# Blank rows for the whole area of the experts' rows, written during attention; reciprocals one reduce later

## The chip, the cores and the metric

The kernel runs on one core of a Trainium2 chip. The metric is the device time of one execution in microseconds (us); less is better. The times before come from three timed runs, the profile from one more execution that was recorded.

## What is computed

The reference is a gated cross-attention followed by a gated mixture of experts, in float32, over 16 slices of 128 rows with 512 columns:

```python
x = x + jnp.tanh(g_xattn[0]) * _L0_xattn_ref(_layernorm(x), ctx, ctx, gamma)
x = x + jnp.tanh(g_ffn[0])   * _L0_ffn_ref(_layernorm(x), ...)

# attention: B=16, 8 heads of 16 rows, 512 queries and 512 keys each
sm = softmax(einsum('bhdq,bhdl->bhql', qh, kh) / sqrt(16)); ret = einsum('bhql,bhdl->bhdq', sm, vh)

# experts: 2048 tokens, 8 experts of hidden size 256..1024, the best 2 of each token
h = x @ down_w + down_b
logits = x @ router_w + router_b - COST_LAMBDA * cost
topv, topi = top_k(softmax(logits), 2); gate = softmax(topv)
out = sum over the two of gate * (gelu(gelu(h * mask) @ w1 + b1) @ w2 + b2)      # every expert's constant term counts
out = (out + 0.1 * shared(h)) @ up_w + up_b + (gelu(x) @ core_w + core_b)
```

## The kernel before

**Attention.** It runs in windows `w`, one for each of the 16 slices, and three more at the ends, here numbered by `w`. In a window TensorE makes 16 score blocks `nat` (L536), the k-th of 0 to 15; VectorE takes the maximum of each (`tensor_reduce`, L707) and, between two of those, does the small jobs of the table `PLACED` (L663): the normalization's statistics of the next slice, the reciprocals `rc` of the softmax sums of two slices ago (L696, behind k = 5), and the statistics of x1. ScalarE takes the exponentials (L632), GpSimd all the slice-wide arithmetic. Windows 4 to 13 are a hardware loop whose body holds two windows.

SyncE issues nearly every transfer of attention, in the order of `sync.body`, from one hardware queue: a transfer waits in program order behind all that stands before it. A window's order is: X (L408), the softmax sums to DRAM (L440), a piece of the weights of 800 KB (L420), the sums back as `dc` (L446), xr, ctx (L416), the k rows to scratch (L467, L468), the k stack of head group 0 from scratch (L396), the reciprocals to scratch (L466), the q rows to scratch, the reciprocals spread (L477), the q stack of group 0 (L396), u and x1 rows out, both stacks of group 1, a block of zeros for the experts' sums (L1177). Each read from scratch waits for the landing of what was written to scratch. The stacks of group 0 have to be in place before the next window's first `nat`.

**Feed-forward.** Four rounds r = 0 to 3 of four slices each: TensorE transposes, multiplies by `down_w`, the router, the shared expert and the core; VectorE selects the two experts of each token and ranks it, and GpSimd scatters each token's row of 1088 bytes to its place in `g_rows` with indirect DMAs (L2042, eight in a round). `g_rows` has for each of the 8 experts a region of 2304 rows, and behind them the unused block of 256 rows. The order on each engine is the hand-written list in `seq`. In the last round the totals of the experts come out of a small matmul (`tot`, L1388) as `nz` (L1571), from which VectorE works out tables of 42 blocks (L1786 to L1878): which rows (`ro`), which weights (`wo`), which biases (`bo`).

An expert's last block of 256 rows reaches past its tokens. So that these rows are harmless (zeros, with an index that adds to rows nobody reads), SyncE writes 256 blank rows behind each expert's count: `fillers` (L1199), eight times a register load of the count `nz` and a DMA of 272 KB, and once for the unused block (L1214). The blank rows stand in `u`, which VectorE clears at the start of the last round (L1976, L1978).

**Expert blocks.** For each of 42 blocks SyncE loads 256 rows transposed (L1240) and their meta columns (L1244); first it waits for `ro`, then in `all_rows_out` for every scatter and blank write. TensorE makes two layers of matmuls (L1295), ScalarE GELU (L1641), VectorE the low parts and the gates, GpSimd adds the rows to `y_sums`. ScalarE's first step there waits for all stores of xb (`t_xs`, L1630). At the end the sums are read back, multiplied by `up_w` and stored.

## Time and profile before

| | |
|---|---|
| timed runs | 732.62, 732.62, 734.15 us; median 732.62 us |
| profiled execution, device time | 740.14 us |
| its span, first to last instruction | 738.0 us |
| busy share: TensorE, VectorE, ScalarE, GpSimd | 93%, 71%, 73%, 65% |
| granted TensorE clock, mean | 0.995 of full speed |
| moved by DMA | 123.98 MB, 168 GB/s |

Stages on the span's clock: lead-in to about 15 us, attention to about 370 us, the four rounds to about 475 us, expert blocks to about 700 us, the end to 738 us. The profiled execution is 7.5 us longer than the median of the timed ones; 2.1 us of it lie around the span, which each execution has some of.

### The profile page before, as it was taken

What the parts mean: (1) busy time and instruction counts of PE and PEld (TensorE: products, weight loads), DVE (VectorE), ACT (ScalarE), POOL (GpSimd) and SP (SyncE); (2) the same over time, 40 slices, a digit from 0 to 9 for tenths busy, and PEclk for the clock granted to TensorE, in tenths of its full rate; (3) what the DMA queues carried; (4) which work ended last, traced back from release to release, by engine and by line L of the source; (5) the groups of instructions that cost most, each with busy time, mean ns of one, the idle gap of its engine ahead of it and who ended that gap; (6) DMA issues with size and microseconds to landing.
All of it is one profiled execution on the core that took longest, in us unless ns stands there. A gap on an engine that the chain in (4) does not pass through costs nothing.

```text
span 738.0 us, 20869 instructions
## 1 busy us (share of the span) xinstructions
PE 687.9 (93%) x6101; PEld 373.1 (51%) x6101; DVE 525.0 (71%) x853; ACT 541.0 (73%) x1129; POOL 480.7 (65%) x474
## 2 busy tenths in 40 slices
PE   1799998999999999999989999799999999999988
PEld 0122222232333333322355544588888888888744
DVE  3989998899999999998877756544444444444456
ACT  2399999899999999999885665487676666767411
POOL 3558788888888898985477244046666666656623
PEclk9999999999999999999999999999999999999999
DMA  6656666656655666545255635599988888887487
GB/s 201 199 151 196 199 207 217 197 175 208 209 192 186 208 207 220 177 139 182 93 166 182 210 118 175 147 172 174 126 119 121 118 135 106 108 102 94 56 250 277
DMA packets 136865, 123.98 MB, mean 168 GB/s; under 512 B 70612, under 2 KB 106196, under 8 KB 136792
## 3 DMA queue, kind: packets, MB, share of 16 engines
q1 hardware_dynamic: 121928, 106.58, 50.4%
q0 software_dynamic: 13632, 15.47, 14.7%
q10 hardware_dynamic: 1232, 0.98, 0.5%
q8 instruction: 41, 0.67, 0.4%
q14 instruction: 32, 0.26, 0.1%
HBM read 60.33 MB, written 51.53 MB: 152 GB/s over the span
## 4 chain that ended last, share of the span: by engine, by line
PE 71%; DVE 10%; DMA 7%; issue 5%; ACT 3%; SPq 3%; POOL 1%; ACTq 0%; DVEq 0%; POOLq 0%
PE EH L1295 25%; PE Y L1295 16%; PE pv L561 12%; PE ring L548 8%; DVE mx L707 6%; PE nat L536 5%; ACT P L632 2%; DMA k_scratch<-khl 1%; DMA QS<-mrow 1%; DVE statx L688 1%; PE ring L580 1%; DMA q_scratch<-qhl 1%; SPq L396 1%; PE ring L571 1%; DMA y_sums<-ysb,to 1%
## 5 line engine op out<-in xcount | busy, mean ns | idle before, releaser
L707 DVE TENSOR_REDUCE mx<-nat 128x2 f32<-128x1024 f32 x256 | 296.8, 1213 | 23.2 <-PE nat L536 22.3
L632 ACT ACTIVATE P<-ring 128x512 f32<-128x512 f32 x512 | 279.4, 603 | 19.8 <-PE ring L548 9.8
L2091 POOL DMA_INDIRECT y_sums<-ysb,to x84 | 138.4, 1647 | 101.6 <-DVE ysb L2028 88.5
L561 PE MATMUL pv<-P,VT 128*32 128x256 f32 x2048 | 158.7, 394 | 0.4
L536 PE MATMUL nat<-KS,QS 48*128 48x512 f16 x512 | 111.8, 397 | 24.4 <-DMA QS<-q_scratch 15.1
L548 PE MATMUL ring<-QS,KS 49*128 49x512 f16 x512 | 123.5, 392 | 9.1 <-ACT P L632 8.5
L1641 ACT ACTIVATE X<-EH,bcur 128x256 f32<-128x256 f32 x168 | 85.6, 559 | 50.9 <-DVE u L1992 27.0
L1295 PE MATMUL Y<-whi,u 128*128 x672 | 117.1, 273 | 0.5 <-DVE u L1992 0.5
L1295 PE MATMUL EH<-XA,whi 128*128 128x256 f16 x672 | 116.9, 273 | 0.3 <-DMA XA<-g_rows 0.3
L1992 DVE TENSOR_TENSOR u<-X,u 128x512 f16<-128x512 f32 x84 | 57.7, 687 | 78.3 <-ACT u L1647 76.5
L1295 PE MATMUL Y<-wlo,u 128*128 x336 | 91.6, 273 | 0.0
L1295 PE MATMUL EH<-XA,wlo 128*128 128x256 f16 x336 | 91.6, 273 | 0.0
L561 PEld LDWEIGHTS pv<-P,VT 128*32 128x32 f32 x2048 | 44.2, 109 | 91.7 <-issue 45.4
L548 PEld LDWEIGHTS ring<-QS,KS 49*128 49x128 f16 x512 | 32.4, 93 | 112.3 <-ACT P L632 95.6
L1295 PEld LDWEIGHTS Y<-whi,u 128*128 128x128 f16 x672 | 65.7, 98 | 8.8 <-issue 1.3
L1295 PEld LDWEIGHTS EH<-XA,whi 128*128 x672 | 65.7, 98 | 8.5 <-issue 1.0
L2028 DVE TENSOR_TENSOR ysb<-Y,gcur 128x512 f32<-128x512 f32 x42 | 29.0, 691 | 46.6 <-PE Y L1295 46.6
L1647 ACT CAST u<-X 128x512 f16<-128x512 f32 x84 | 51.9, 618 | 7.3 <-ACT X L1641 0.4
L536 PEld LDWEIGHTS nat<-KS,QS 48*128 48x128 f16 x512 | 26.0, 94 | 37.7 <-DVE mx L707 21.5
L1295 PEld LDWEIGHTS Y<-wlo,u 128*128 128x128 f16 x336 | 32.9, 98 | 3.8
L1295 PEld LDWEIGHTS EH<-XA,wlo 128*128 x336 | 32.9, 98 | 3.8
L1655 ACT CAST uh<-Y 128x256 f16<-128x256 f32 x16 | 6.0, 372 | 32.3 <-PE Y L1508 32.3
(266 smaller groups left out, 995.4 us busy)
## 6 DMA issues: line engine op xcount, KB each, us to landing
XA<-in_wall SPq DMA_DIRECT2D x8, 800.0 KB, 4.4
u<-in_wall SPq DMA_DIRECT2D x8, 800.0 KB, 4.4
QS<-q_scratch SPq DMA_DIRECT2D x64, 96.0 KB, 2.5
KS<-k_scratch SPq DMA_DIRECT2D x62, 96.0 KB, 2.2
X<-in_x SPq DMA_DIRECT2D x16, 256.0 KB, 2.8
q_scratch<-qhl SPq DMA_DIRECT2D x16, 256.0 KB, 2.1
xr<-in_x SPq DMA_DIRECT2D x16, 256.0 KB, 3.7
rd<-den_scratch SPq DMA_DIRECT2D x16, 256.0 KB
```

The costliest lines, as they stand in the source:

```text
L396: sp.dma_start(dst[HALF * a:HALF * a + K_QK, g, :, :], src).then_inc(t_stk[g][b % 2].sem, 16)
L536: m = pe.matmul(nat[k % 2][:, a, :], QS[i][r, g, n, q0:q0 + P], KS[i][r, g, n, :], start=True, stop=True)
L548: pe.matmul(ring[place[key] % 3][:, :], KS[i][r, g, n, lb * P:lb * P + P], QS[i][r, g, n, :], start=True, stop=True).then_inc(t_ring.sem, 1)
L561: m = pe.matmul(pv[32 * j:32 * j + 32, q], VT[i][:, lb, g, j, :], Pb[4 * (s % 2) + j][:, q], start=(lb == 0 and half == 0), stop=(lb == 3) ...
L632: act.activation(Pb[4 * (s % 2) + j][:, :], bank[:, :], ACT.Exp).then_inc(t_use.sem, 1)
L707: dve.tensor_reduce(mx[:, k // 8, :, k % 8], nat[k % 2][:, :, :], AX.X, ALU.max).then_inc(t_max.sem, 1)
L1295: m = pe.matmul(dst, l, r, start=first and n == 0, stop=last and n == 2, skip_group_check=skip)
L1641: m = act.activation(af[j % 2][:, tile, :], EH[j % 2][:, n, s * BLK:(s + 1) * BLK], ACT.Gelu, bias=bcur[:, j % 2, tile:tile + 1], scale=bc ...
L1647: act.copy(ah[j % 2][:, 2 * n:2 * n + 2, :], af[j % 2][:, 2 * n:2 * n + 2, :]).then_inc(t_ah.sem, 1)
L1992: dve.tensor_tensor(al[j % 2][:, 2 * n:2 * n + 2, :], af[j % 2][:, 2 * n:2 * n + 2, :], ah[j % 2][:, 2 * n:2 * n + 2, :], ALU.subtract).th ...
L2028: dve.tensor_tensor(ysb[j % 2][:, :, :], EY[j % 2], gcur[:, j % 4, :].unsqueeze(2).broadcast_to([P, 2, LAT]), ALU.mult).then_inc(t_dve.sem, 1)
L2091: pool.indirect_dma_start(out=ysum[:, :], out_offset=bass.IndirectOffsetOnAxis(ap=to[:, j % 2, a:a + 1], axis=0), in_=ysb[j % 2][:, a, :], ...
```

## The change

The blank rows move from `u` into a tile of their own, `blank` (two rows of 1088 bytes in each partition, 2176 bytes), of which `zs` and `Z` become parts. GpSimd clears it at the very start in place of `zs`; in window 2 a small DMA writes the two index columns, which now come from the constants. In each of the windows 3 to 14 SyncE writes 1536 rows of `g_rows` in two halves of 128 x 3 x 2176 bytes (816 KB each): half 0 between the k rows' stores and the k stack of group 0, half 1 at the window's end. After 12 windows all 18432 rows of the eight regions are blank; window 15 writes the unused block (272 KB). `fillers`, the block write of L1214 and VectorE's clearing in the last round are gone; the scatters of round 0 wait for all blank writes (`t_zr`), and so does the first later use of `zs` as something else. The reciprocals go from behind k = 5 to behind k = 6, ahead of x1's statistics, both behind the same reduce.

```diff
-            "gb": sb("gb", [P, NT]), "zs": sb("zs", [P, LAT]), "Z": sb("Z", [P, LAT]),
+            "gb": sb("gb", [P, NT]), "blank": sb("blank", [P, ROW]),
         }
+        keep["zs"], keep["Z"] = (keep["blank"][:, k * ROW // 2:k * ROW // 2 + LAT] for k in range(2))
...
                     sp.dma_start(scr[ck.index(b), :, 2], hl[b % 2][:, high, :]).then_inc(t_.sem, 16)
+                    if side == 1 and 3 <= w < B - 1:
+                        tail["blank rows"](ck, w, 0)
                     if side == 1:
                         stack(ck, b, 0, 1)
...
             if 3 <= w < B:
                 tail["zeros"](ck, w)
+            if 3 <= w < B - 1:
+                tail["blank rows"](ck, w, 1)
+            if w == B - 1:
+                tail["unused block"]()
...
-        PLACED = {1: ("stats",), 2: ("aggr",), 5: ("recip",), 6: ("xstats",), 7: ("xaggr",)}
+        PLACED = {1: ("stats",), 2: ("aggr",), 6: ("recip", "xstats"), 7: ("xaggr",)}
...
-                    if todo and (todo[0][1] in PLACED.get(k, ())):
+                    while todo and todo[0][1] in PLACED.get(k, ()):
...
-                pool.memset(keep["zs"][:, :], 0.0).then_inc(t_vt.sem, 1)
+                pool.memset(keep["blank"][:, :], 0.0).then_inc(t_vt.sem, 1)
...
-    blank = flat(u)[:, 0:ROW].rearrange("p (a c) -> p a c", a=2)
+    blank = keep["blank"][:, :].rearrange("p (a c) -> p a c", a=2)
+    by_window = gsc[0:DUMP, :].rearrange("(w h j p a) c -> w h p j (a c)", h=2, j=3, p=P, a=2)
...
+        def blank_in():
+            sp.dma_start(blank[:, :, LAT:LAT + META],
+                         const[:, NCONST + K2_BLANK:NCONST + K2_BLANK + 2 * META].rearrange("p (a c) -> p a c", a=2)).then_inc(t_bl.sem, 16)
+
+        def blank_rows(ck, w, half):
+            if w == 3:
+                sp.wait_ge(t_bl.sem, 16)
+            sp.dma_start(by_window[ck.index(w - 3), half],
+                         blank[:, :, :].rearrange("p a c -> p (a c)").unsqueeze(1).broadcast_to([P, 3, ROW])).then_inc(t_zr.sem, 16)
+
+        def unused_block():
+            sp.dma_start(gsc[DUMP:DUMP + BLK, :].rearrange("(p a) c -> p (a c)", a=2),
+                         blank[:, :, :].rearrange("p a c -> p (a c)")).then_inc(t_zr.sem, 16)
...
-            def fillers():
-                wait(sp, t_act, NG - 1, "nz", 0)
-                for e in range(E):
-                    v = sp.value_load(nz[0:1, e:e + 1], min_val=0, max_val=ROWS)
-                    region = gsc[e * REGION:(e + 1) * REGION, :]
-                    sp.dma_start(blocks(region[bass.ds(v, BLK), :]), blank).then_inc(t_zr.sem, 16)
...
-                if r == NG - 2:
-                    sp.wait_ge(t_zd.sem, 10)
-                    sp.dma_start(blocks(gsc[DUMP:DUMP + BLK, :]), blank).then_inc(t_zr.sem, 16)
...
-                    if r == NG - 2 and t == 0:
-                        fillers()
...
-                sp.wait_ge(t_zr.sem, 16 * (E + 1))
+                sp.wait_ge(t_zr.sem, t_zr.value)
...
                         act.wait_ge(t_dz.sem, t_dz.value)
+                        act.wait_ge(t_zr.sem, t_zr.value)
...
-                if r == NG - 1:
-                    wait(dve, t_pe, 2, "uT", LB - 1)
-                    dve.memset(blank, 0.0).then_inc(t_zd.sem, 1)
-                    dve.wait_ge(t_zd.sem, 9)
-                    dve.tensor_copy(blank[:, :, LAT + META - 1], cs2[:, K2_DUMP:K2_DUMP + 2]).then_inc(t_zd.sem, 1)
...
+                if (r, i) == (0, 0):
+                    pool.wait_ge(t_zr.sem, t_zr.value)
```

On SyncE's queue, window 3 from its ctx load to the loop's start. Before:

```order
L416 DMA X<-in_ctx_kv 128x512
L467 DMA k_scratch<-khl 128x1024
L468 DMA k_scratch<-khl 128x512
L396 DMA KS<-k_scratch 48x2x512 x2
L466 DMA den_scratch<-rc 128x32
...
L396 DMA QS<-q_scratch 48x2x512 x2
L1174 DMA y_sums<-zs 128x2x256 x2
L1177 DMA y_sums<-zs 128x256 x4
L377 UNCONDITIONAL_BRANCH
```

After (`y_sums<-blank` is the same write of zeros, out of the new tile):

```order
L417 DMA X<-in_ctx_kv 128x512
L468 DMA k_scratch<-khl 128x1024
L469 DMA k_scratch<-khl 128x512
L1198 DMA g_rows<-blank 128x3x544
L397 DMA KS<-k_scratch 48x2x512 x2
L467 DMA den_scratch<-rc 128x32
...
L397 DMA QS<-q_scratch 48x2x512 x2
L1186 DMA y_sums<-blank 128x2x256 x2
L1189 DMA y_sums<-blank 128x256 x4
L1198 DMA g_rows<-blank 128x3x544
L378 UNCONDITIONAL_BRANCH
```

Two transfers of 816 KB have come in, one behind the k rows' stores and one behind the zeros; nothing else has changed places.

On VectorE, window 3 from the next slice's statistics on. Before:

```order
L682 BN_STATS stats<-X 128x6
L707 TENSOR_REDUCE mx<-nat 128x2
L685 BN_AGGR mv<-stats 128x2
L707 TENSOR_REDUCE mx<-nat 128x2 x3
L696 RECIPROCAL rc<-dc 128x32
L707 TENSOR_REDUCE mx<-nat 128x2
L688 BN_STATS statx<-ao 128x6
L707 TENSOR_REDUCE mx<-nat 128x2
L692 BN_AGGR mvx<-statx 128x2
```

After:

```order
L691 BN_STATS stats<-X 128x6
L716 TENSOR_REDUCE mx<-nat 128x2
L694 BN_AGGR mv<-stats 128x2
L716 TENSOR_REDUCE mx<-nat 128x2 x4
L705 RECIPROCAL rc<-dc 128x32
L697 BN_STATS statx<-ao 128x6
L716 TENSOR_REDUCE mx<-nat 128x2
L701 BN_AGGR mvx<-statx 128x2
```

The reciprocal has moved behind one more reduce and stands directly ahead of x1's statistics.

## Rows read from the trace of the kernel before

**Rows 1.** Two stretches: length, engines' busy us, granted clock, DMA share, GB/s

```profile
40.00:345.00 305.00, 292.16 (x2896) 90.03 (x2893) 288.06 (x300) 282.35 (x584) 253.51 (x285) 0.99 0.61 194
500.00:600.00 100.00, 100.00 (x918) 89.63 (x917) 43.11 (x76) 69.63 (x154) 63.10 (x39) 1.00 0.88 131
```

**Rows 2.** A group of DMA issues: count, KB each, us to landing, the page

```profile
XA<-in_wall SPq DMA_DIRECT2D x8, 800.0 KB, 4.4
```

**Rows 3.** VectorE in one window of the loop: start, us, line, what

```profile
252.78 0.34 DVE L696 RECIPROCAL rc<-dc 128x32 f32<-128x32 f32 x1
...
255.93 11.41 DVE L707 TENSOR_REDUCE mx<-nat 128x2 f32<-128x1024 f32 x10
267.25 0.69 DVE L682 BATCH_NORM_STATS2 stats<-X 128x6 f32<-128x512 f32 x1
```

**Rows 4.** SyncE's queue in the same window: start, us of issue, line, transfer

```profile
247.05 0.34 SPq L420 DMA_DIRECT2D XA<-in_wall  x1
248.01 0.34 SPq L446 DMA_DIRECT2D dc<-den_scratch  x1
...
259.39 0.84 SPq L396 DMA_DIRECT2D QS<-q_scratch  x2
```

**Rows 5.** Stretches of the same window, columns as in rows 1

```profile
246.00:248.00 2.00, 2.00 (x23) 0.63 (x17) 1.89 (x3) 1.81 (x5) 1.90 (x3) 1.00 0.16 60
248.00:254.00 6.00, 6.00 (x60) 1.98 (x60) 5.25 (x7) 5.57 (x14) 5.08 (x9) 1.00 0.87 293
254.00:255.00 1.00, 1.00 (x13) 0.21 (x5) 1.00 (x3) 0.86 (x3) 0.76 (x2) 1.00 0.00 0
```

**Rows 6.** SyncE's queue in window 4, the loop's first

```profile
100.95 0.34 SPq L446 DMA_DIRECT2D dc<-den_scratch  x1
...
113.16 1.14 SPq L396 DMA_DIRECT2D QS<-q_scratch  x2
```

**Rows 7.** VectorE in window 4; in brackets its idle us and what ended it

```profile
104.35 0.35 DVE L696 RECIPROCAL rc<-dc 128x32 f32<-128x32 f32 x1 [0.25 <-DMA dc<-den_scratch]
...
117.63 2.36 DVE L707 TENSOR_REDUCE mx<-nat 128x2 f32<-128x1024 f32 x2 [0.98 <-PE nat L536]
```

**Rows 8.** Stretches of window 4, columns as in rows 1

```profile
98.00:101.00 3.00, 3.00 (x29) 1.04 (x28) 2.97 (x4) 2.82 (x8) 2.85 (x4) 1.00 0.45 121
101.00:106.00 5.00, 5.00 (x52) 1.51 (x52) 4.01 (x5) 4.58 (x11) 3.99 (x9) 1.00 0.92 324
```

**Rows 9.** The last round, SyncE: blank writes (all eight, and one alone), first load

```profile
451.32 13.76 SPq L1203 DMA_DIRECT2D g_rows<-u  x8
...
460.31 0.00 SPq L1203 DMA_DIRECT2D g_rows<-u  x1
...
472.39 1.37 SPq L1240 DMA_TRANSPOSE XA<-g_rows  x1
```

**Rows 10.** The last round, VectorE

```profile
458.34 0.57 DVE L1800 TENSOR_TENSOR hc<-hc 128x8 f32<-128x8 f32 x3
464.75 0.75 DVE L1920 SCALAR_TENSOR_TENSOR X<-EH,gate,X 128x512 f32<-128x512 f32 x1 [5.84 <-PE Y L1409]
```

**Rows 11.** The chain that ended last, in order of time: start, us, what

```profile
456.27 5.18 PE EH L1295 x24
...
463.60 1.09 issue
464.69 5.36 PE EH L1295 x24
...
471.84 1.28 DVE sal L1902 x2
...
474.94 2.83 DMA xb_rows<-X
...
479.03 1.03 ACT X L1641 x2
```

**Rows 12.** A stretch of the last round, columns as in rows 1

```profile
458.00:465.00 7.00, 5.68 (x34) 3.14 (x33) 1.02 (x6) 0.97 (x2) 3.84 (x4) 1.00 0.59 199
```

## What the change should do, and why

> **What bounds the kernel now.** I read the stretches first [rows 1]. In attention TensorE, VectorE and ScalarE are all busy for 93 to 96% of 305 us, and the DMA engines for 0.61: what is added to an engine there costs at once, while transfers have room, as long as nobody waits for one that stands behind them. In the expert blocks TensorE alone is full (100.00 of 100.00 us). So the 9 small writes that go were never part of a full engine's work, and the question is where a transfer's end releases someone: in attention the order of SyncE's queue [rows 4, 6], in the last round the path from the counts to the first expert block [rows 9 to 11].
>
> **The size of what comes.** A half is 128 x 3 x 2176 bytes = 816 KB, as much as a piece of the weights (800 KB), which takes 4.4 us from issue to landing [rows 2]. Over 5 us in which the queue is never empty the core moves 324 GB/s at a share of 0.92 [rows 8], so 0.836 MB take 0.836 / 324 x 1000 = 2.6 us at that pace, and 2.4 us at a full share. Two halves in 12 windows are 20.1 MB against 2.5 MB that go. In a window of 20.7 us this is 4.8 us more, 0.23 of share: 0.61 becomes 0.84. They fit on average.
>
> **Half 1 in a window of the loop.** It stands ahead of the sums' store, whose landing SyncE awaits before it reads dc. The DMA engines are nearly idle from 246 to 248 (share 0.16), 1.7 us, just where half 1 would run [rows 5]. Of 2.4 us some 0.7 are left over, plus about 0.5 us for one more issue (an issue takes 0.34 to 0.45 us here [rows 4]) and 0.5 for X and the sums that move behind it: dc is issued some 1.7 us later than 248.01 and lands that much later at the most. The reciprocal at 252.78 did not wait; behind k = 6 it stands one reduce later, and a reduce takes 1.14 us here (11.41 / 10), so at about 254.2 with the gaps [rows 3], 1.4 us later. Since the dc packets stood behind 800 KB of weights anyway, the delay is less than the issue's. I take no wait; the bounds are 0 and 0.5 us a window.
>
> **Half 0 in a window of the loop.** It stands behind the k rows' stores and ahead of the k stack. The DMA engines are idle from 254 to 255 (share 0.00) while the k rows' landing is awaited [rows 5]: 1 us of 2.4 is free, about 1.4 us pass to the k stack and the q rows, less what their own waits give back. The q stack is issued at 259.39 + 0.84 [rows 4]. It is needed at the next window's k = 0: ten reduces from 255.93 to 267.25 at 1.14 each, of which the last two are the next window's, so at 265.0 [rows 3]. Even with the 4.4 us of the 800 KB piece it lands at 264.6; small reads take less. 1.4 us fit. Cost 0, with the same bound of 0.5 us a window.
>
> **Window 4 is different.** There the q stack is late already: VectorE waits 0.98 us for the first `nat` and starts at 117.63, and the reciprocal waits 0.25 us for dc [rows 7]. The reason is window 3, which writes six blocks of zeros at once: SyncE issues dc at 100.95, sits on the landings of what stands behind it, and issues the q stack only at 113.16 [rows 6]. Half 1 of window 3 stands behind those zeros. From 98 to 101 the share is 0.45 [rows 8], so 1.65 us are free, of which I count 1.2 (the rest comes after dc's turn); 1.2 us stay, and 0.5 of issue. Half 0 of window 4 runs while the k rows' landing is awaited, at no cost but an issue. So the q stack is 1.0 to 1.7 us later and nothing hides it, since it is the last to arrive: **+1.3 us, once**. The reciprocal there would stall some 0.5 us; it lies ahead of the same wait and is not added. Bounds: 0 (if the stores come through sooner) and +2.6 (a full half).
>
> **The reciprocals.** Moved, not added: 0.34 us stay 0.34 us. In windows 15 and later its store to scratch stands behind it on SyncE, but also behind 2 MB of loads; nothing.
>
> **The waits that come.** ScalarE before `zs` is overwritten and GpSimd before the first scatter wait for writes issued 25 us earlier: 0. GpSimd's first clearing grows from 256 to 544 columns, a few tenths in the lead-in beside VectorE's chain: 0 to +0.3, I take 0.1.
>
> **The last round.** VectorE's clearing (some 0.6 us) at its start is beside TensorE's matmuls: 0. SyncE's part is more: eight reads of the counts with a write each from 451.32 for 13.76 us [rows 9]. Their end is not awaited by the load at 472.39, which comes 2 us behind `ro`. But during them something odd stands in the trace. VectorE is done with `hc` at 458.91 and should go on with the core's sum of the second slice, whose 12 matmuls are the first half of the 24 from 456.27 and end at 458.9 [rows 10, 11]; it starts at 464.75, after 5.84 us [rows 10], put down to a matmul that is not its own. ScalarE and SyncE too go on only then, and TensorE has 1.09 us of idle with no releaser up to 464.69 [rows 11]. The DMA engines are at 0.59 meanwhile [rows 12]: it is no lack of bandwidth. If it goes with the fillers, then: TensorE starts its 24 matmuls at 463.60 in place of 464.69 and ends them at 469.0; `sal`, which stands 7.1 us behind 464.75 in VectorE's own order (471.84), would stand at 466.1 by that, or at 467 where ScalarE decides, so before 469.0; the last two steps of the shared expert follow without their wait from 470.05 to the end of the first `sal` at 472.5, so 1.1 + 2.4 = 3.5 us are won on TensorE [rows 11]. ScalarE's wait for the last xb store (474.94 + 2.83) moves with TensorE and VectorE by 4 to 4.5 us, and so does its first GELU at 479.03. The first output matmuls stand behind both and come some 3.8 us earlier, and from there TensorE is full: **-3.8 us**, bounds -3.5 and -4.5. If it does not go, or stands only in the recorded execution: 0.
>
> Whether the timed runs have this halt the profile can't say. The profiled execution is 7.5 us longer than their median, and a halt with all its effects is 4 to 6 us of just this sort. Within it SyncE's write at 460.31 stands with 0.00 us, where an issue takes 0.34 us and more [rows 4, 9]: that looks like records held up, not like work. So I take it as part of the recording. The Trainium skill bears on it from both sides. "NOTIFIC — the notification-queue block", section 7.1, says that the block that writes a profile's records holds engines up rather than lose a record inside it; by that the halt is the recorder's, no row here shows the block itself, and the timed gain is nothing. "Runtime: NRT & Kernel Launch", section on the preamble and postamble, gives a gap of about 6.2 us between a profile's total and the execution time for any kernel; an estimate by that page leaves 1.3 us of the 7.5 for the halt, which would then be real and the gain nearly whole. The two disagree, and no run here decides.
>
> **The sum.** Window 4 +1.3, lead-in +0.1, last round -0.2 (SyncE and the DMA engines less loaded, no row that a full engine waits on): +1.2 us. The median 732.6 becomes **733.8 us**. In the recording the halt should go as well: 740.1 + 1.2 - 3.8 = 737.5.
>
> **The rivals.**
> - The halt is real and the fillers make it. Then 732.6 + 1.3 + 0.1 - 3.8 = 730.2; with both bounds 728.2 to 731.7. For it: three engines stand still at once in the span in which SyncE does the count reads. Against it: a shorter one stands in the round before, without fillers, and the above.
> - The other side: the halves also cost in each window of the loop, through dc or the q stack. It decides from the point at which a landing comes later by more than the 1.4 us that the reciprocal gained, or the q stack by more than the 2 us and more up to 265.0. VectorE then stands in 10 to 11 windows for 0.3 to 1 us: +3 to +10, with window 4 about 739 us. For it: a mean share of 0.84 lengthens every landing. Against it: the gaps above.
> - The change does nothing measurable: window 4's wait is absorbed by later idle time of others, or the blank halves run where nobody waits: 732.5.
>
> **Chances.** Forecast (733.0 to 735.3) 0.50: about two thirds of it within 0.2%, which is 1.5 us and about what a measurement of this kernel can tell from no change, the rest above. Halt real and gone 0.28, of which 0.24 is faster by over 0.2%. Cost in each window 0.14, all slower. Nothing 0.08. So faster 0.24, within 0.2% 0.43 (0.32 of the forecast, 0.04 of the halt, 0.07 of nothing), slower 0.33. The range that holds 8 in 10 goes from 729.4 to 737.5: it takes in nearly all of the real halt and the lighter end of the cost in each window. The likeliest case has 733.0 to 735.3 of its own.
>
> **What would show it.** After, VectorE's idle time before the first reduce of window 5 should be 2 to 3 us, and once; elsewhere the reciprocal should have no DMA as its releaser. The DMA share of attention should be 0.80 to 0.86. The core's sum on VectorE behind `hc` should come within 0.3 us. If it does and the timed runs are about 4 us faster, the halt was real and my step on the recording is wrong. If attention's stretch grows by more than 3 us, the gaps were misread.

## The result and the profile after

The changed kernel takes **739.78 us** in the median of four runs (738.32 to 740.94), the kernel before 733.38 us beside it: ratio 1.0092, interval 1.0076 to 1.0108. It is 6.4 us slower. I had forecast 733.8 us with 737.5 as the upper end, so the time lies outside the range, on the side of the rival that costs in attention. The recorded execution has a device time of 738.32 us and a span of 736.1 us. That is shorter than the 740.14 us recorded for the kernel before, and both signs are explained below.

The columns of the stretches are those of [rows 1]. The first line is attention, the second the expert blocks:

```profile
40.00:345.00 305.00, 288.58 (x2836) 87.99 (x2832) 282.94 (x296) 276.89 (x572) 248.45 (x281) 0.98 0.79 258
...
500.00:600.00 100.00, 100.00 (x918) 89.63 (x917) 43.21 (x77) 69.05 (x152) 63.32 (x39) 1.00 0.91 131
```

In the same 305 us TensorE is busy 3.6 us less than in [rows 1], VectorE 5.1 us less, ScalarE 5.5 us less, and the DMA share is 0.79 where it was 0.61. The expert blocks are as before. So attention lost time. Its end can be read from one row of each kernel, all 256 reduces of VectorE (shortest/median/longest in ns, first and last start in us); before stands first, then after:

```profile
L707 DVE TENSOR_REDUCE mx<-nat x256: 1162/1217/1228, 14.4 to 346.4; 128x2 f32<-128x1024 f32 x128
```

```profile
L716 DVE TENSOR_REDUCE mx<-nat x256: 1160/1215/1229, 14.2 to 351.6; 128x2 f32<-128x1024 f32 x128
```

The last start is 5.2 us later. The statistics of the next slice stand in each window behind k = 1 and serve as a clock. VectorE before, windows 4 to 8:

```profile
97.86 0.68 DVE L682 BATCH_NORM_STATS2 stats<-X 128x6 f32<-128x512 f32 x1
119.91 0.68 DVE L682 BATCH_NORM_STATS2 stats<-X 128x6 f32<-128x512 f32 x1
142.17 0.68 DVE L682 BATCH_NORM_STATS2 stats<-X 128x6 f32<-128x512 f32 x1
163.23 0.68 DVE L682 BATCH_NORM_STATS2 stats<-X 128x6 f32<-128x512 f32 x1
184.38 0.68 DVE L682 BATCH_NORM_STATS2 stats<-X 128x6 f32<-128x512 f32 x1
```

VectorE after, the same with the reciprocals, in brackets the idle time and what ended it:

```profile
97.82 0.68 DVE L691 BATCH_NORM_STATS2 stats<-X 128x6 f32<-128x512 f32 x1
107.98 0.35 DVE L705 RECIPROCAL rc<-dc 128x32 f32<-128x32 f32 x1 [2.79 <-DMA dc<-den_scratch]
122.76 0.68 DVE L691 BATCH_NORM_STATS2 stats<-X 128x6 f32<-128x512 f32 x1
144.39 0.68 DVE L691 BATCH_NORM_STATS2 stats<-X 128x6 f32<-128x512 f32 x1
151.93 0.35 DVE L705 RECIPROCAL rc<-dc 128x32 f32<-128x32 f32 x1 [0.89 <-DMA dc<-den_scratch]
168.15 0.68 DVE L691 BATCH_NORM_STATS2 stats<-X 128x6 f32<-128x512 f32 x1
188.87 0.68 DVE L691 BATCH_NORM_STATS2 stats<-X 128x6 f32<-128x512 f32 x1
```

Window 4 takes 24.94 us in place of 22.05, window 6 takes 23.76 in place of 21.06; windows 5 and 7 are 0.63 and 0.43 us shorter than before. That makes 4.5 us at window 8, and 0.7 us come later. In this record the loss is not spread over the loop: it sits in two windows, and in both VectorE stands at the reciprocal for `dc`, which is late. The kernel before is not the whole measure, though. With the reciprocals alone moved (`recip_only` below) window 4 takes 23.49 us and window 6 takes 20.71, and attention ends at 345.9. Beside that kernel the blank rows cost 5.7 us of attention, 1.45 of them in window 4 and 3.05 in window 6.

**How `dc` becomes late.** SyncE in window 4, start and us of issue:

```profile
97.47 0.46 SPq L1198 DMA_DIRECT2D g_rows<-blank  x1
...
99.09 1.89 SPq L441 DMA_DIRECT2D den_scratch<-U  x2
101.35 0.35 SPq L421 DMA_DIRECT2D u<-in_wall  x1
103.45 0.33 SPq L447 DMA_DIRECT2D dc<-den_scratch  x1
```

Half 1 of window 3 is the first line. `dc` is issued at 103.45 where [rows 6] has 100.95: 2.5 us later, about the whole transfer of a half. The chain that ended last goes through just this:

```profile
100.43 2.75 DMA den_scratch<-U
103.45 4.42 DMA dc<-den_scratch
108.89 1.13 DVE mx L716
110.45 1.39 PE pv L570 x16
```

**What the wait sets off.** TensorE, with its idle time in brackets, and two stretches:

```profile
110.06 0.39 PE L545 MATMUL nat<-KS,QS 48*128 48x512 f16 x2 [2.99 <-DVE mx L716]
...
113.05 1.08 PE L570 MATMUL pv<-P,VT 128*32 128x256 f32 x8
...
114.72 0.64 PE L570 MATMUL pv<-P,VT 128*32 128x256 f32 x8
```

```profile
111.00:115.00 4.00, 4.00 (x37) 0.71 (x25) 2.72 (x4) 1.85 (x4) 3.67 (x4) 0.58 0.49 160
152.00:156.00 4.00, 2.59 (x23) 0.83 (x24) 4.00 (x6) 2.62 (x6) 2.72 (x6) 0.91 1.00 349
156.00:160.00 4.00, 4.00 (x26) 0.67 (x24) 2.73 (x3) 2.38 (x5) 3.62 (x4) 0.50 0.51 163
```

The reduces stand behind the reciprocal in VectorE's order and the next `nat` behind the reduces, so TensorE stands for 2.99 us. Then its granted clock falls: eight `pv` matmuls take 1.08 us in place of 0.64, and the mean over 111 to 115 us is 0.58. In window 6 the wait is only 0.89 us, but TensorE was busy for 2.59 of 4 us and from 156 to 160 it runs at 0.50, the lower level of 1.2 GHz. Window 6 is 2.7 us longer than before, three times the wait. What the clock alone costs can be read from two of the kernels below, `both` and `half1_only`, of which each waits once for `dc` in its window 12, 1.89 and 1.79 us. The stretch behind the wait, `both` first:

```profile
284.00:288.00 4.00, 4.00 (x49) 1.25 (x41) 4.00 (x5) 2.91 (x6) 3.58 (x4) 1.00 0.49 158
```

```profile
284.00:288.00 4.00, 4.00 (x25) 0.67 (x24) 2.85 (x3) 2.55 (x5) 3.52 (x4) 0.50 0.51 161
```

With the clock at 1.00 the window takes 22.96 us, with the fall to 0.50 it takes 25.09, 2.1 us more for a wait that is no longer. So a wait of a given length has no one price: whether the clock falls behind it decides, and these records do not show what decides that.

**The last round.** The core's sum behind `hc` on VectorE, as in [rows 10]:

```profile
461.91 0.57 DVE L1815 TENSOR_TENSOR hc<-hc 128x8 f32<-128x8 f32 x3
462.51 0.75 DVE L1935 SCALAR_TENSOR_TENSOR X<-EH,gate,X 128x512 f32<-128x512 f32 x1
```

The halt of 5.84 us is gone. The span is 1.9 us shorter although attention ends 5.2 us later, so 7.1 us are won behind attention. They go with the halt and not with the fillers as such: `recip_only`, which has all the fillers and in its record no halt, takes 384.6 us from the last reduce's start to the end of its span, the changed kernel 384.5, the kernel before 391.6. The recorded executions differ by +5.2 and -7.1 us, the timed ones by +6.4.

### The profile page after: what moved, and what is told of

Same layout as the page of the kernel before. It is cut to its first block, busy times and chain, and to the rows that moved or that the text cites. A ratio compares the mean times of both kernels' runs of the same rounds, so it can differ in the third digit from the quotient of the medians.

```text
span 736.1 us, 20885 instructions
## 1 busy us (share of the span) xinstructions
PE 688.5 (94%) x6101; PEld 372.8 (51%) x6101; DVE 524.8 (71%) x851; ACT 541.1 (74%) x1129; POOL 481.1 (65%) x474
## 4 chain that ended last, share of the span: by engine, by line
PE 76%; DVE 9%; DMA 5%; issue 4%; SPq 3%; ACT 2%; POOL 0%; DVEq 0%; ACTq 0%; POOLq 0%
PE EH L1309 27%; PE Y L1309 17%; PE pv L570 13%; PE ring L557 9%; DVE mx L716 6%; PE nat L545 5%; ACT P L641 2%; DMA k_scratch<-khl 1%; DMA dc<-den_scratch 1%; PE ring L589 1%; DVE statx L697 1%; SPq L397 1%; DMA q_scratch<-qhl 1%; PE ring L580 1%; DMA QS<-q_scratch 1%
## 5 line engine op out<-in xcount | busy, mean ns | idle before, releaser
L749 POOL TENSOR_TENSOR ao<-tn,rd 128x512 f32<-128x512 f32 x16 | 20.3, 1269 | 14.8 <-DMA rd<-den_scratch 14.7
```

Source lines behind the costliest of these rows:

```text
L749: done(pool.tensor_tensor(ao[i][:, :], tn[:, :], rd[:, :], ALU.mult))
```

## The experiments

Each session timed its kernels beside the kernel before. Medians differ between sessions (before: 733.5, 732.9, 738.8, 738.1 and 733.6 us), so ratios are read within one. "Last reduce" is the last start of the row quoted twice above, from the recorded execution, which for each kernel of this table is one of its timed runs.

| kernel | last reduce, us | median, us | ratio to before | interval | before |
|---|---|---|---|---|---|
| recip_only | 345.9 | 732.75 | 0.9990 | 0.9972 to 1.0008 | 733.53 |
| both | 352.9 | 739.47 | 1.0082 | 1.0055 to 1.0110 | 733.53 |
| half0_only | 346.7 | 732.66 | 0.9985 | 0.9966 to 1.0004 | 733.53 |
| half1_only | 355.1 | 737.55 | 1.0061 | 1.0038 to 1.0083 | 733.53 |
| half1_moved | 358.6 | 743.79 | 1.0152 | 1.0121 to 1.0184 | 732.87 |
| recip_at_8 | 348.9 | 738.35 | 1.0079 | 1.0056 to 1.0102 | 732.87 |
| dc_first | 358.2 | 745.28 | 1.0155 | 1.0119 to 1.0192 | 732.87 |
| moved_dc_first | 378.9 | 765.08 | 1.0436 | 1.0405 to 1.0467 | 732.87 |
| late_zeros | 342.9 | 734.97 | 0.9942 | 0.9914 to 0.9969 | 738.75 |
| after_late_zeros | 349.1 | 739.59 | 0.9998 | 0.9965 to 1.0031 | 738.75 |
| on_scalar_queue | 382.2 | 768.87 | 1.0381 | 1.0329 to 1.0433 | 738.75 |
| tiny_halves | 346.0 | 737.89 | 1.0001 | 0.9972 to 1.0029 | 738.75 |
| window3_spared | 349.2 | 738.97 | 1.0013 | 0.9988 to 1.0037 | 738.08 |
| recip_at_5 | 354.6 | 743.28 | 1.0077 | 1.0044 to 1.0110 | 738.08 |
| zeros_only | 345.8 | 734.24 | 0.9948 | 0.9923 to 0.9973 | 738.08 |
| after_again | 350.4 | 739.58 | 1.0030 | 1.0004 to 1.0056 | 738.08 |
| reads_kept | 354.5 | 738.50 | 1.0073 | 1.0047 to 1.0098 | 733.57 |
| writes_kept | 353.6 | 740.09 | 1.0082 | 1.0055 to 1.0108 | 733.57 |

### One part at a time

The reciprocals alone, on the kernel before:

```diff
-        PLACED = {1: ("stats",), 2: ("aggr",), 5: ("recip",), 6: ("xstats",), 7: ("xaggr",)}
+        PLACED = {1: ("stats",), 2: ("aggr",), 6: ("recip", "xstats"), 7: ("xaggr",)}
```

> The kernel before, with the reciprocals behind k = 6 as in the changed kernel and nothing else changed. Theory (a wait of VectorE for the softmax sums `dc` is what costs in attention, through TensorE behind it and its clock): the two waits of the reciprocal in windows 4 and 5 (0.25 and 0.78 us in the trace of before) go, and with them the dip of the granted clock at 128 to 136 us; TensorE's 1.37 us of lag at 133 us is won, so 0.7 to 1.5 us faster than before, and attention in the record 0.7 to 1.5 us shorter. Rival (the move of the reciprocals is itself what lengthens attention, by holding GpSimd's normalization back): slower than before by 1 to 5 us.

The other three are the changed kernel with the fillers put back beside the blank rows of attention (`both`), and of that only half 0 or only half 1 in each window:

```diff
 # both; half0_only also leaves out the second call, half1_only the first
+            def fillers():
+                wait(sp, t_act, NG - 1, "nz", 0)
+                for e in range(E):
+                    v = sp.value_load(nz[0:1, e:e + 1], min_val=0, max_val=ROWS)
...
+                    sp.dma_start(blocks(region[bass.ds(v, BLK), :]), late_blank).then_inc(t_zf.sem, 16)
-                        tail["blank rows"](ck, w, 0)
-                tail["blank rows"](ck, w, 1)
```

> The changed kernel with the fillers of the kernel before put back as well (eight reads of the counts with a write of 272 KB each, the unused block, VectorE's clearing of `u`), beside the blank rows of attention. Theory (the halt of 5.84 us belongs to that one recorded execution and the fillers cost nothing where nothing is recorded): as the changed kernel, 739.8 us, within 1 us. Rival (the halt is real, and its removal paid back a part of what attention costs): 3.8 to 6.8 us slower than the changed kernel, 743.5 to 746.5 us. For both attention in the record is about 5 us longer than before.

> As the kernel before this one in the list (fillers kept), but without half 1 in each window, so half of the area gets blank rows only from the fillers, as in the kernel before. Theory (half 1 ahead of the sums' stores makes `dc` late): `dc` is issued as early as before, the reciprocals do not wait, attention is within 1 us of the one with the reciprocals alone moved, and the time 732 to 734.5 us. Rival (it is the load on the DMA engines, whatever the place): half of the loss, about 3 us slower than before.

> Fillers kept, half 1 in each window kept, half 0 left out. Theory: `dc` is issued about 2.5 us later in window 4 and the reciprocal waits for it; all of the loss of attention is here, 4 to 6 us, about 738 to 740 us. Rival (load, whatever the place): about 3 us slower than before, and no difference from the kernel with half 0 alone.

Half 0 costs nothing that can be measured, and half 1 alone costs 4.0 us, where both together cost 5.9 (the intervals overlap). The first waits of the reciprocal with half 1 alone (none stand in the record with half 0 alone):

```profile
106.60 0.35 DVE L704 RECIPROCAL rc<-dc 128x32 f32<-128x32 f32 x1 [0.92 <-DMA dc<-den_scratch]
129.95 0.35 DVE L704 RECIPROCAL rc<-dc 128x32 f32<-128x32 f32 x1 [1.11 <-DMA dc<-den_scratch]
151.79 0.35 DVE L704 RECIPROCAL rc<-dc 128x32 f32<-128x32 f32 x1 [0.54 <-DMA dc<-den_scratch]
```

`dc` is issued at 101.21 us with half 0 alone and at 103.64 with half 1 alone, 2.4 us apart. The rival that only the load counts is out: the bytes are the same. The reciprocals alone moved cannot be told from no change (0.9990); the gain of 0.7 to 1.5 us that I expected is not there in the recorded attention either (0.5 us). The two waits for `dc` did go, but another has grown. VectorE at window 5's start, with nothing written to `g_rows` in attention:

```profile
118.70 2.36 DVE L707 TENSOR_REDUCE mx<-nat 128x2 f32<-128x1024 f32 x2 [2.67 <-PE nat L536]
```

TensorE waits there for the q stack, where the kernel before has 0.98 us [rows 7]; with half 0 alone it is 3.34 us. Why the stack comes later in these records stays open. By its ratio (1.0082, the changed kernel 1.0092) `both` is as slow as the changed kernel although it has all fillers, so in that session the fillers cost nothing.

The blank rows without the move of the reciprocals, and the changed kernel again beside it:

```diff
-        PLACED = {1: ("stats",), 2: ("aggr",), 6: ("recip", "xstats"), 7: ("xaggr",)}
+        PLACED = {1: ("stats",), 2: ("aggr",), 5: ("recip",), 6: ("xstats",), 7: ("xaggr",)}
```

> The changed kernel with the reciprocals back behind k = 5, so the blank rows alone. Theory: each wait for `dc` begins one reduce (1.14 us) earlier and ends at the same time, so window 4's is about 3.9 us and window 6's about 2 us, and the steady windows, in which `dc` landed 1.5 to 2 us before the reciprocal, keep 0.4 to 0.9 us of room: 1 to 3 us slower than the changed kernel. Rival (the reciprocals' place is of no weight): within 0.15% of it.

> The changed kernel once more, to stand beside the three others in one session. Theory: 0.8 to 1.0% slower than before, with the wait of some 2 to 2.8 us for `dc` in window 4 and one of about 1 us in window 6; attention ends about 5 us later than in before.

With the reciprocals at k = 5 the kernel is 3.7 us slower than the changed one in the same session (743.28 against 739.58), more than the 1 to 3 us expected: there are five waits for `dc` in place of three, 6.8 us in place of 2.6, one of them of 2.45 us in window 8, where the changed kernel had none. The move hides a part of what the blank rows do. `after_again` waits 1.72 us in window 4 and 0.56 in window 6, less than the first record, and attention ends 4.0 us later than before. Its window 4 takes 26.42 us all the same, more than the 24.94 of the first record, since TensorE then stands at 0.50:

```profile
108.00:112.00 4.00, 3.82 (x27) 1.06 (x31) 2.47 (x5) 0.65 (x2) 3.08 (x6) 0.50 0.85 281
```

Its ratio of 1.0030 missed the 0.8 to 1.0% expected; its time is the same as in the first session, and it is the kernel before that is 5 us slower here (below).

### Bytes or issues

The changed kernel with the fillers put back, and each half cut to 64 bytes in each of 128 partitions:

```diff
-            sp.dma_start(by_window[ck.index(w - 3), half],
-                         blank[:, :, :].rearrange("p a c -> p (a c)").unsqueeze(1).broadcast_to([P, 3, ROW])).then_inc(t_zr.sem, 16)
+            sp.dma_start(by_window[ck.index(w - 3), half][:, 0, 0:16], blank[:, 0, 0:16]).then_inc(t_zr.sem, 16)
```

> The kernel with both the fillers and the halves, with each half cut to 64 bytes of each of 128 partitions: the same number of issues at the same places of SyncE's queue, 8 KB in place of 816 KB (the fillers still write all that is needed). Theory (bytes ahead of an awaited landing cost, not issues): within 0.3% of the kernel with the reciprocals alone moved, 732 to 734.5 us, and no wait for `dc` above 0.3 us. Rival (SyncE has no time for two more issues in a window): 736 to 739 us.

No reciprocal waits in attention, which is as long as with the reciprocals alone moved (346.0 and 345.9 us). Two more issues in a window cost nothing; their bytes ahead of an awaited landing do. The time of 737.89 us is outside the 732 to 734.5 us expected, for the session's kernel before was at 738.75; the ratio of 1.0001 fits.

### Another place, another queue

Half 1 behind the q stack of group 0; the read of the sums ahead of the weights (on the kernel before with the reciprocals moved); both together:

```diff
             if 0 <= w and b < B:
                 stack(ck, b, 0, 0)
+            if 3 <= w < B - 1:
+                tail["blank rows"](ck, w, 1)
...
                 tail["zeros"](ck, w)
-            if 3 <= w < B - 1:
-                tail["blank rows"](ck, w, 1)
```

```diff
-            if 2 <= w < B - 1:
-                load_weights(ck, w + 1)
...
                 sp.dma_start(dc[:, :], sd[ck.index(t), 0].rearrange("h (s q) -> (h s) q", s=P // NH)).then_inc(t_dc.sem, 16)
+            if 2 <= w < B - 1:
+                load_weights(ck, w + 1)
```

> The changed kernel with half 1 at another place in each window: behind the q stack of group 0 in place of behind the zeros at the window's end, with the same bytes. Theory (the place of half 1 ahead of the sums' store is the whole loss): `dc` is issued in window 4 as early as with half 0 alone (at about 101 us), no reciprocal waits, attention's end is within 1.5 us of before, and the time 732 to 735 us. Rival (load: 20 MB more in attention cost what they cost, wherever they stand): 738 to 740 us as the changed kernel, or waits of VectorE for `nat` in more windows, since the stacks of group 1 come later.

> The kernel before with the reciprocals behind k = 6 and the sums' read `dc` ahead of the piece of the weights; fillers as before, no blank rows in attention. Theory: SyncE waits some 2 us for the sums' stores with an idle queue, but `dc` no longer stands behind 800 KB and lands 1.5 to 2 us earlier; since no reciprocal waited in the kernel with the reciprocals alone moved, nothing is won: 732.0 to 733.5 us. Rival (what follows the idle 2 us, ctx, k rows and k stack, is late next): 1 to 4 us slower.

> The changed kernel with half 1 behind the q stack of group 0 and the sums' read ahead of the piece of the weights. Theory: as with half 1 moved alone, within 1 us of it, with more room before each reciprocal: 732 to 735 us. Rival (the queue is too full for another idle stretch): VectorE waits for `nat` at the starts of windows, 1 to 5 us slower than with half 1 moved alone.

All three went against me. Moving half 1 makes eight waits for `dc` of 7.7 us in all in attention, in place of two of 3.7 us. The half still stands ahead of the sums in the same queue, only further ahead, and now also ahead of u, x1 and the stacks of group 1. So "the place behind the zeros is the whole loss" is false; what counts is the queue's backlog wherever the half stands ahead of the sums.

`dc_first` shows the other end of the same queue. It has no waits for `dc` in attention and is the slower by 12 us. SyncE in its window 10:

```profile
233.15 1.33 SPq L440 DMA_DIRECT2D den_scratch<-U  x2
235.91 0.34 SPq L444 DMA_DIRECT2D dc<-den_scratch  x1
...
239.14 0.35 SPq L468 DMA_DIRECT2D k_scratch<-khl  x1
244.09 1.10 SPq L396 DMA_DIRECT2D KS<-k_scratch  x2
```

SyncE stands 1.4 us for the sums' landing with an idle queue, then the weights, xr and ctx go ahead of the k rows, and the k stack is issued 4.6 us behind them, where the kernel before has 1.9 us in its window 11. TensorE waits for the q stack eight times in attention, and so VectorE for `nat` at the windows' starts, once 5.09 us:

```profile
121.81 2.36 DVE L707 TENSOR_REDUCE mx<-nat 128x2 f32<-128x1024 f32 x2 [5.09 <-PE nat L536]
```

The rival came true and beyond its 1 to 4 us. SyncE's queue is a ring of landings that closes once a window, with little room at each, not the 39% that the DMA share leaves: in window 11 of the changed kernel `dc` is issued at 254.19 us, takes 3.1 us in the median to land, and the reciprocal stands at 258.96, so 1.7 us are left.

Both halves on ScalarE's queue, each behind its row of maxima:

```diff
-                        tail["blank rows"](ck, w, 0)
-                tail["blank rows"](ck, w, 1)
                     if row:
                         max_row(ck, *row)
                         row = None
+                        if 3 <= w < B - 1:
+                            tail["blank rows"](ck, w, halves.pop(0))
```

> The changed kernel with both halves of each window issued by ScalarE, each behind its row of maxima, in place of SyncE: the same bytes to the same places, on another queue. Theory (order and landings on SyncE's queue are what costs): no transfer of SyncE's stands behind 816 KB, so `dc` is issued as early as before; two issues of about 0.5 us on ScalarE lie beside its own work: 732 to 736 us. Rival (load on the 16 DMA engines, whose share is 0.82 either way): reads that somebody waits for share the engines with the halves, and it stays at 738 to 742 us.

The theory "order on SyncE's queue is all" fell, and so did the size of its rival: 3.8% slower. Issues of DMA in the changed kernel and here (KB each, median us to landing):

```profile
g_rows<-blank SPq DMA_DIRECT2D x24, 816.0 KB, 4.6
...
k_scratch<-khl SPq DMA_DIRECT2D x15, 256.0 KB, 2.9
```

```profile
g_rows<-blank ACTq DMA_DIRECT2D x24, 816.0 KB, 5.5
...
k_scratch<-khl SPq DMA_DIRECT2D x15, 256.0 KB, 4.6
```

The k rows land 1.7 us later, most likely since they can now run beside a half instead of standing ahead of it, and `dc` is waited for eight times in attention, 10.1 us. The Trainium skill, "DMA: Bandwidth & Descriptors", section "Issuing engines are not separate DMA queues", says that DMAs of different engines run on the same 16 DMA engines and interleave; the rows agree. How much of the 30 us is ScalarE's own time for the issues was not separated.

### Where the loss starts

The reciprocals and x1's statistics behind k = 8:

> The changed kernel with the reciprocals and x1's statistics behind k = 8 in place of k = 6, and the aggregation behind k = 9; the blank rows stay where they are. Theory (VectorE stands behind a late `dc`, and TensorE behind VectorE): two reduces of 1.14 us each move ahead of the wait, so of the 2.79 us in window 4 some 0.5 us stay and the 0.89 us of window 6 go; the clock does not fall at 108 to 116 and 152 to 164 us; 3 to 5 us of the 5.2 us come back: 735 to 737 us. Rival (what costs is the late reciprocal itself, through the spread copy `rd` and GpSimd's normalization that `ao`, the low parts and the next q rows stand behind): no gain or slower, 739 to 743 us.

```profile
107.54 0.35 DVE L705 RECIPROCAL rc<-dc 128x32 f32<-128x32 f32 x1 [0.68 <-DMA dc<-den_scratch]
...
118.91 2.36 DVE L716 TENSOR_REDUCE mx<-nat 128x2 f32<-128x1024 f32 x2 [2.50 <-PE nat L545]
```

The wait for `dc` is 0.68 us and alone, as expected, and now a wait for the q stack shows, 2.50 us at window 5's start against 0.98 in [rows 7]. It looks like the one that I had forecast, but it can't be put down to half 1, since `recip_only` has 2.67 us there without any blank rows. And TensorE waits for the q stack at the starts of eight more windows, 0.8 to 1.5 us each, where the changed kernel has one such wait. With the wait for `dc` out of the way the queue's next awaited landing bounds the window. It is not that the q stack stands behind a late reciprocal: in window 11 the reciprocal is at 257.60 us and its store, behind the k stack, at 259.82. SyncE's whole window lies later against VectorE's (`dc` is issued 4.2 us behind the next slice's statistics, 2.6 in the changed kernel); why is open. The recorded attention ends 2.7 us earlier than the changed one. But the ten timed runs, from 734.9 to 741.1 us, have their median at 738.35: outside the 735 to 737 us, and by its ratio 0.1% better than the changed kernel, which is within the intervals. The record is of the fastest of them, so it is no guide to the median.

Half 1 of window 3 left out there and written in window 15:

```diff
-            if 3 <= w < B - 1:
+            if 4 <= w < B - 1:
                 tail["blank rows"](ck, w, 1)
             if w == B - 1:
                 tail["unused block"]()
+                tail["blank rows"](ck, 3, 1)
```

> The changed kernel without half 1 of window 3; its rows are written beside the unused block in window 15, everything else as in the changed kernel. Theory (the transient of windows 4 to 6 starts with half 1 of window 3, queued behind six writes of zeros and ahead of the sums): `dc` of window 4 is issued at about 101 us as before, the wait of 2.79 us goes, and 2 to 4 us of the 5.2 us of attention come back: 0.3 to 0.6% faster than the changed kernel in the same session. Rival (window 5's half 1 makes the same backlog one window later, so the wait only moves): within 0.15% of the changed kernel, with a wait for `dc` of over 1 us in window 5 or 6.

```profile
104.84 0.34 DVE L706 RECIPROCAL rc<-dc 128x32 f32<-128x32 f32 x1
...
128.96 0.35 DVE L706 RECIPROCAL rc<-dc 128x32 f32<-128x32 f32 x1 [2.50 <-DMA dc<-den_scratch]
```

The rival is right: the wait moves to window 5 with 2.50 us. The time is within 0.1% of `after_again`. What one half 1 is spared, the next one pays.

So I took away what stands ahead of it in window 3. Of its six writes of zeros five were moved to window 15 (two of 256 KB and three of 128 KB, 896 KB in all; the window's own stays), on the changed kernel and on the kernel before with the reciprocals moved, and on the kernel before alone:

```diff
             if w == 3:
                 sp.wait_ge(t_vt.sem, 4)
-                tail["spare zeros"]()
-                for n in range(3):
-                    tail["zeros"](ck, n)
             if 3 <= w < B:
                 tail["zeros"](ck, w)
+            if w == B - 1:
+                tail["spare zeros"]()
+                for n in range(3):
+                    tail["zeros"](ck, n)
```

> The kernel before with the reciprocals behind k = 6 and the six writes of zeros of window 3 (L1174 twice, L1177 for windows 0 to 2 three times, and the spare blocks) moved to the end of window 15; fillers kept, no blank rows in attention. Theory (SyncE's queue is one chain of issues and landings that takes nearly a whole window; what six writes delay in window 3 is paid in windows 4 and 5): windows 4 and 5, which take 23.5 and 21.5 us with the reciprocals alone moved, take 20.7 to 21 us, so 2.5 to 3.6 us of attention are won: 729 to 731 us. Rival (window 4 is late because the hardware loop begins there, whatever the queue holds): 732.5 us, no change. What speaks against a gain in full: two more writes beside 2 MB of loads in window 15, up to 0.5 us.

> The changed kernel (blank rows in attention, no fillers) with the same six writes of zeros moved to the end of window 15. Theory: the 2.79 us wait of the reciprocal in window 4 goes to under 0.5 us and most of the transient behind it, 3 to 5 us of the 5.2 us: 734 to 737 us. Rival (the windows of the loop lose in any case, since half 1 and half 0 leave the queue no room): 739 to 741 us.

> The kernel before with only the six writes of zeros moved from window 3 to window 15; reciprocals behind k = 5. Theory: as with both moves (0.6% faster than before), since no reciprocal waits once the zeros are gone: 0.4 to 0.6% faster than before. Rival (both moves are needed): 0.1 to 0.3% faster, with a wait for `dc` in windows 4 or 5.

`late_zeros` ends attention 3.0 us earlier than `recip_only` (342.9 against 345.9) and has no wait for `dc`. `after_late_zeros` ends it 2.5 us earlier than the changed kernel in its first record and 1.3 us earlier than in its second. Its time is unchanged against before (0.9998), where `after_again` stood at 1.0030 in the next session, and the intervals overlap: a gain on the changed kernel is not shown, and the 3 to 5 us that I expected are out. The rival, that the loop loses in any case, held. The blank rows cost 6.2 us of recorded attention with the zeros moved (349.1 against 342.9) and 5.7 with the zeros in place (351.6 against 345.9), and 0.6% of the time between the two kernels of the one session. So the zeros of window 3 are a loss of their own and not what makes half 1 cost. No reciprocal waits in window 4 now, and `dc` is waited for twice, 1.3 us together; TensorE waits for other small transfers instead, 1.4 us for a q stack in window 6 and, in window 4, for the row of maxima that ScalarE sends:

```profile
104.68 0.49 PE L557 MATMUL ring<-QS,KS 49*128 49x512 f16 x2 [1.47 <-DMA QS<-mrow]
```

The clock falls behind this wait as well, to a mean of 0.66 from 104 to 108 us. That transfer is not on SyncE's queue, so the order of that queue cannot be all of the loss; how the rest of it divides was not separated. The best versions are those without blank rows in attention: zeros moved, 0.9948 with the reciprocals at k = 5 and 0.9942 at k = 6, about 4 us faster than before and 5 us faster than the changed kernel. Both were timed only in sessions in which the kernel before takes 738 us. `late_zeros` missed the 729 to 731 us that I expected (734.97) in such a session. The zeros are enough; the reciprocals' place adds nothing that can be told. The record of `zeros_only` ends attention at 345.8 for another reason: it lost some 3 us in window 1, ahead of anything changed, and its windows 4 and 5 take 20.7 us each.

### The halt of the last round

Nine records have all the fillers, and the halt between `hc` and the core's sum of [rows 10] parts them. The kernel before has it (5.84 us), `tiny_halves`, `late_zeros` and `zeros_only` have it (4.22, 2.83 and 2.81 us), and of `recip_only`, `both`, `half0_only`, `half1_only` and `dc_first`, none has it. No record without fillers has it, in any session. Fillers and the sum, `recip_only` first, then `tiny_halves`:

```profile
449.23 9.95 SPq L1203 DMA_DIRECT2D g_rows<-u  x8
```

```profile
456.25 0.57 DVE L1800 TENSOR_TENSOR hc<-hc 128x8 f32<-128x8 f32 x3
456.85 0.75 DVE L1920 SCALAR_TENSOR_TENSOR X<-EH,gate,X 128x512 f32<-128x512 f32 x1
```

```profile
450.20 13.65 SPq L1231 DMA_DIRECT2D g_rows<-u  x8
```

```profile
457.22 0.57 DVE L1830 TENSOR_TENSOR hc<-hc 128x8 f32<-128x8 f32 x3
462.01 0.75 DVE L1950 SCALAR_TENSOR_TENSOR X<-EH,gate,X 128x512 f32<-128x512 f32 x1 [4.22 <-PE Y L1438]
```

Beside the first record of the kernel before, whose own device time is 740.14 us, the halts stand in the two sessions in which the kernel before takes 738 to 739 us, and the five records without one in the two at 733; the changed kernel takes 739.6 to 739.8 us in either kind. The three recorded executions with a halt are timed runs themselves and lie -0.1, +1.2 and +1.3 us from the medians of their kernels (`tiny_halves`, `late_zeros`, `zeros_only`). So the halt is most likely in the other timed runs of these sessions too; they were not recorded, so this is inferred from the medians. Where it occurs, the change gives back some 5 us and costs 0.3%; where it does not, 0.9%. The last two kernels keep one part of the fillers each, on the changed kernel, to see which makes it:

```diff
 # reads_kept: a write of 64 bytes behind each read of a count
-                    sp.dma_start(blocks(region[bass.ds(v, BLK), :]), late_blank).then_inc(t_zf.sem, 16)
+                    sp.dma_start(region[bass.ds(v, 1), 0:16], late_blank[0:1, 0, 0:16]).then_inc(t_zf.sem, 16)
 # writes_kept: the bytes to fixed rows, no reads
-                    v = sp.value_load(nz[0:1, e:e + 1], min_val=0, max_val=ROWS)
-                    sp.dma_start(blocks(region[bass.ds(v, BLK), :]), late_blank).then_inc(t_zf.sem, 16)
+                    sp.dma_start(blocks(region[ROWS:ROWS + BLK, :]), late_blank).then_inc(t_zf.sem, 16)
```

> The changed kernel with, in the last round, the eight reads of the counts of the kernel before and a write of 64 bytes behind each (and the unused block of 272 KB), in place of the eight writes of 272 KB. The question is the halt of the last round: between two fixed matmuls of that round (the 840th and the 900th behind attention's last reduce) stand 9.13 to 9.14 us in every record without fillers, 9.13 or 9.14 in five with them, and 10.6 to 13.7 in four with them (before among these). Theory 1 (2.2 MB in 10 us beside the reads of xb, u and the scatters hold up the semaphores of the engines): no halt, 9.14 us. Theory 2 (SyncE's register reads of the counts, out of a tile in SBUF, make it): 10.6 us or more if the session is one with halts, in which the kernel before stands near 738 us and not 733. With the kernel before at 733 us neither is told apart. The time is the changed kernel's, 739 to 741 us, plus the halt.

> The changed kernel with the eight writes of 272 KB of the last round kept, but to fixed rows (the last 256 of each expert's region), without the reads of the counts. Theory 1 (the bytes make the halt): 10.6 us or more between the same two matmuls in a session with halts, 1.5 to 4.5 us slower than the kernel with the reads kept. Theory 2 (the reads make it): 9.14 us. In a session with the kernel before at 733 us both stand at 9.14 us.

The session was one without halts (before at 733.57 us), and neither shows one. What they do show is that the eight reads, not the bytes, take SyncE's time: 9.68 us for the fillers with the reads and 64 bytes each, 5.60 with the full bytes and no reads. Which part makes the halt stays open, and so does what is different in the sessions that have it. It is not the chip alone: the session at 733.5 us and the one at 738.1 us ran on the same one.

## Why the prediction was wrong

- **What bounds the kernel**: right. Attention is full on three engines, and what an engine there waits for is paid at once.
- **The size of a half and the share of the DMA engines**: right within a little. 2.6 us at full pace, measured 2.4 to 2.5 us of delay; 0.80 to 0.86 of share forecast, 0.79 measured.
- **Half 0**: right, 0 us (`half0_only`).
- **Half 1 in a steady window of the loop**: right within a little for the record of the result, 0.7 us from window 8 on. The room is thin, though, and the rival is partly right: other records of kernels with half 1 have a single wait for `dc` of 1.8 to 2.45 us in window 8 (`recip_at_5`, `writes_kept`) or 12 (`both`, `half1_only`), and such a window is 2.25 to 4.7 us longer.
- **Window 4, the step that failed.** I gave half 1 a free 1.2 us of the nearly idle stretch 98 to 101 and put `dc` 1.7 us later; it came the full 2.5 us later, since the queue was never empty behind the zeros. Then I called the reciprocal's stall "some 0.5 us" and did not add it, as it "lies ahead of the same wait". It is 2.79 us in the first record and 1.72 in the second, and it is what VectorE and TensorE pay. The q stack is issued 1.3 us later, as I had it (its issue ends at 115.60 us, 114.30 in [rows 6]), but nobody waits for it in window 5 any more, and half 1 is not shown as the reason: in `recip_only`, without blank rows, it ends at 115.82. So no run shows the +1.3 us of the sum as a cost of half 1; that the number is near the 1.45 us by which window 4 is longer than in `recip_only` is luck.
- **The clock, the term that was missing.** A wait of VectorE that left TensorE idle was followed by 0.50 of the clock, 1.2 GHz, from 156 to 160 us in the first record and from 108 to 116 us in the second. In window 6 a wait of 0.89 us cost 2.7. The pair in window 12 puts the fall at 2.1 us, and it does not follow every wait. The trace of before held the price already, behind a wait of 0.78 us for `dc` in its window 5, and I did not use it:

```profile
128.00:132.00 4.00, 3.03 (x23) 0.87 (x20) 3.74 (x5) 2.01 (x5) 2.21 (x6) 0.71 0.35 108
```

  Window 6 was not in my sum at all: I had "once".
- **The reciprocals at nothing**: right on the kernel before (0.9990), wrong on the changed one, where the later place is worth 3.7 us. Later still is no better: at k = 8 the q stack is waited for nine times.
- **The last round.** For the session of the result I was right to give it no timed gain. As a statement on what the halt is I was wrong: it is not the recorder's alone. The Trainium skill's "NOTIFIC — the notification-queue block", section 7.1, on which one of my two readings leaned, cannot tell it. The same recorder leaves nine records with fillers, four with the halt and five without. The other reading leaned on the Trainium skill's "Runtime: NRT & Kernel Launch", section "The ~15µs preamble/postamble breakdown", and its 6.2 us between profile and execution. Here the recorded executions of the result and of the experiments are timed runs, at 738.32 us for a median of 739.78 in the changed kernel and at 732.68 for 732.75 in `recip_only`, so no such gap lies between a recorded time and a timed one, and the 6.2 us had no place in the 7.5. Device time less span is 1.8 to 2.2 us in all records.
- **The rivals.** The one on the other side named the right resource (`dc`) and nearly the right time, 739 us, at a chance of 0.14, but as a small cost in each window. In the record of the result it was two windows and the clock. The real halt, at 0.28, exists as well, in other sessions than that of the result.

## What to carry to other kernels

A share of 0.61 on the DMA engines is no measure of room on a queue in which landings are awaited: follow each awaited landing through the windows, count every byte that stands ahead of it since the queue was last empty, and look first at the window in which it is late already. Where an engine at 95% feeds TensorE, price a wait with the clock that may fall behind it, one to three times its length here. Compare with the kernel that has all but one part of the change, not only with the one before: here it showed that a wait put down to half 1 was there without it. And where a trace shows that start-up writes make the queue late, move them: here five writes of zeros, 896 KB, about 4 us. That gain is beside the blank rows' cost and does not remove it.

## What the runs showed of the hardware

- The issue of a transfer by SyncE has no fixed length. In the changed kernel the sums' two stores took 1.89 us in place of 1.33 in window 4 (the share of the DMA engines is 0.99 to 1.03 from 97 to 101 us, and 0.45 from 98 to 101 in [rows 8]), and a pair of q stacks 1.85 us in place of 0.79 at 118.4 us. Full engines are not the only case: in `recip_only` a pair of q stacks took 1.86 us at 113.96 us, with a share of 0.37 and 0.42 in the two microseconds from 113 to 115.
- ScalarE's row of maxima, 4 KB on its own queue, was waited for 1.47 us in `after_late_zeros` and 1.07 us in `window3_spared`.
- The kernel before takes 733 or 738 us according to the session, and the halt of the last round goes with the slower kind. What differs between the sessions was not found.
